# Weight rows shifted by 64 bytes each, two activation slots instead of three, and a signal after each bank of the first layer

## What is computed

```python
def _L0_ffn_ref(x, w1_w, w1_s, ...):          # 256 -> 1024 -> 1024 -> 1024 -> 256
    h = silu(tlin(x, w1_w, w1_s)) * tlin(x, w2_w, w2_s)
    h = gelu(tlin(h, h1_w, h1_s))
    h = gelu(tlin(h, h2_w, h2_s))
    return tlin(h, w3_w, w3_s)
x = x + 0.5 * ffn(layernorm(x))
x = x + attn(layernorm(x))                     # FFT convolution, gelu, @ W.T + b
x = x + 0.5 * ffn(layernorm(x))
```

## Time and profile before

| | |
|---|---|
| median of 3 runs | 1441.88 us (1441.57 to 1443.68) |
| the profiled execution, its own time | 1441.73 us |
| its span, first to last instruction | 1439.9 us |
| mean granted TensorE clock | 1.000 |
| busy: PE / PEld / DVE / ACT / POOL | 1432.2 / 1162.6 / 986.7 / 476.6 / 48.3 us |

### The profile page before, as it was taken

The page is one execution under the profiler, slowest core; times in us unless marked ns, Lnnn a source line. Parts: engine busy times, 40 slices in busy tenths (PEclk is TensorE's granted clock), DMA queues, the critical chain, the costliest instruction groups (busy, mean ns, idle before and its releaser), DMA issues.

```text
span 1439.9 us, 17283 instructions
## 1 busy us (share of the span) xinstructions
PE 1432.2 (99%) x6918; PEld 1162.6 (81%) x6918; DVE 986.7 (69%) x1736; ACT 476.6 (33%) x724; POOL 48.3 (3%) x42
## 2 busy tenths in 40 slices
PE   9999999999999999999999999999999999999999
PEld 4788888888778878788787878878878788888887
DVE  7867867675778887848878587784777754353433
ACT  5524342433324223233242232422424223141331
POOL 0000000000000000010000100001000010000000
PEclk9999999999999999999999999999999999999999
DMA  9000000012113221031210312012120112010000
GB/s 366 16 0 30 30 30 30 16 45 59 41 55 136 67 66 59 25 119 44 88 59 12 132 45 73 30 44 99 59 74 15 59 41 74 1 36 9 30 1 16
DMA packets 53906, 80.28 MB, mean 56 GB/s; under 512 B 2752, under 2 KB 45632, under 8 KB 52544
## 3 DMA queue, kind: packets, MB, share of 16 engines
q1 hardware_dynamic: 53824, 79.15, 16.2%
HBM read 57.12 MB, written 22.02 MB: 55 GB/s over the span
## 4 chain that ended last, share of the span: by engine, by line
PE 97%; DVE 2%; ACT 0%; issue 0%; POOL 0%; DVEq 0%
PE ps L1317 80%; PE ps L1391 8%; PE ps L1442 3%; PE ps L1495 2%; PE ps L1293 1%; PE ps L1436 1%; PE ps L1437 1%; PE ps L1404 1%; PE ps L1485 0%; DVE low L1176 0%; PE ps L1310 0%; DVE hid_b_lo L1211 0%; PE ps L1419 0%; PE ps L1427 0%; DVE hid_b_hi L1209 0%
## 5 line engine op out<-in xcount | busy, mean ns | idle before, releaser
L494 ACT ACTIVATE act_o<-ps,scales 128x512 f32<-128x512 f32 x384 | 264.6, 690 | 911.9 <-PE ps L1317 909.7
L1317 PE MATMUL ps<-hid_b_hi,h 128*128 128x512 f32 x1024 | 401.5, 392 | 0.5 <-DVE hid_b_lo L1211 0.5
L1317 PE MATMUL ps<-hid_b_lo,h 128*128 128x512 f32 x1024 | 398.7, 389 | 0.0
L1317 PE MATMUL ps<-hid_a_hi,h 128*128 128x512 f32 x992 | 391.0, 394 | 0.2
L1317 PE MATMUL ps<-hid_a_lo,h 128*128 128x512 f32 x992 | 386.4, 390 | 0.0
L1317 PEld LDWEIGHTS ps<-hid_b_hi,h 128*128 128x128 f32 x1024 | 192.2, 188 | 42.2 <-issue 1.2
L1317 PEld LDWEIGHTS ps<-hid_b_lo,h 128*128 128x128 f32 x1024 | 192.2, 188 | 40.7 <-issue 1.2
L1317 PEld LDWEIGHTS ps<-hid_a_hi,h 128*128 128x128 f32 x992 | 186.2, 188 | 45.7 <-DVE hid_a_lo L1202 2.4
L1317 PEld LDWEIGHTS ps<-hid_a_lo,h 128*128 128x128 f32 x992 | 186.2, 188 | 39.8 <-issue 2.2
L1317 PE MATMUL ps<-hid_b_hi,w 128*128 128x512 f32 x480 | 189.5, 395 | 0.0
L1317 PE MATMUL ps<-hid_b_lo,w 128*128 128x512 f32 x480 | 188.1, 392 | 0.0
(11 more groups left out here) (268 smaller groups left out, 1269.5 us busy)
## 6 DMA issues: line engine op xcount, KB each, us to landing
ks<-k_d SPq DMA_DIRECT2D x32, 512.0 KB, 3.9
raws<-in_weights SPq DMA_DIRECT2D x10, 1024.0 KB, 15.6
xin<-in_x SPq DMA_DIRECT2D x8, 512.0 KB, 3.9
x_d<-xin SPq DMA_DIRECT2D x8, 512.0 KB, 2.8
z_d<-xin SPq DMA_DIRECT2D x8, 512.0 KB, 2.8
zb<-z_d SPq DMA_DIRECT2D x8, 512.0 KB, 4.7
wb<-x_d SPq DMA_DIRECT2D x8, 512.0 KB, 4.1
x_d<-wb SPq DMA_DIRECT2D x8, 512.0 KB, 3.3
```

The source lines that it names most:

```text
L494: A(act_o[:, k % ACT_SLOTS], bank(source), func, scale=scale).then_inc(s_act, 1)
L1317: last = MM(o, weight[:, k, cols].bitcast(dt), part[:, k].bitcast(dt), start=(k == 0 and i == 0), stop=(k == n - 1 and i == len(act_) - 1))
```

## The change

1. **Rows.** h1, h2 and w3 get 16 more floats (SKEW, 64 bytes) per row, so that row k starts 64 k bytes further into a 512-byte line than row 0. hid_b, and all that lies behind it (xin, act_o, gz, zb, wb, fb, tt, ks, tables), starts 64 bytes into a line. w1, w2 and hid_a stay at line starts. Transfers, checks and roundings of the weights use rows instead of flat runs of 2,048 floats.
2. **Slots.** ACT_SLOTS goes from 3 to 2: ScalarE waits for the gate or split of k - 2.
3. **Signals.** TensorE raises a new semaphore s_half when the w1 bank of step m is full; ScalarE's silu waits for that and no longer for s_u. VectorE's gate waits for s_act and for s_u. TensorE's step m waits for s_act of m - 2 before its w1 product and for s_gate of m - 2 before its w2 product.

```diff
-ACT_SLOTS = 3
+ACT_SLOTS = 2
+
+SKEW = 16
...
+        shapes = {"w1": (KD, HID, 0), "w2": (KD, HID, 0), "h1": (KH, HID, SKEW), "h2": (KH, HID, SKEW), "w3": (KH, D, SKEW)}
...
+        *padded, W0 = zone(FRONT, *((n, [P, k, w + skew], F32R) for n, (k, w, skew) in shapes.items()))
+        r12, rh1, rh2, r3, _ = zone(
+            FRONT, ("raw_12", [P, 2 * KD, HID]), ("raw_h1", [P, KH, HID + SKEW]), ("raw_h2", [P, KH, HID + SKEW]),
+            ("raw_w3", [P, KH, D + SKEW]))
+        w1, w2, h1, h2, w3 = (t[:, :, 0:w] for t, (k, w, skew) in zip(padded, shapes.values()))
...
+        hid_a_hi, hid_a_lo, HB = zone(X0, ("hid_a_hi", [P, KH, TOK], F32R), ("hid_a_lo", [P, KH, TOK], F32R))
+        HB += 4 * SKEW
+        hid_b_hi, hid_b_lo, xin, act_o, gz, Z0 = zone(
...
+        def of_chunk(c, matrices):
+
+            for t in matrices:
+                n = t.shape[1] * t.shape[2] // CHUNK
+                if c < n:
+                    at = t.shape[1] // n
+                    return t[:, at * c:at * (c + 1)]
+                c -= n
+
+        def raw(c):
+            return of_chunk(c, (r12[:, :, :], rh1[:, :, 0:HID], rh2[:, :, 0:HID], r3[:, :, 0:D]))
...
-                    sp.dma_start(raws[:, chunk(c)], a["weights"][:, chunk(c)]).then_inc(s_w[c], 16)
+                    sp.dma_start(raw(c), by_rows(a["weights"][:, chunk(c)], c)).then_inc(s_w[c], 16)
...
             def hidden(T, k, func, scale):
-                act.wait_ge(s_u, at_u(T, k))
+                if k < KH:
+                    act.wait_ge(s_half, at_gate(T, k))
+                else:
+                    act.wait_ge(s_u, at_u(T, k))
...
-                A(place(c), raws[:, chunk(c)], ACT.Copy).then_inc(s_placed, 1)
+                A(place(c), raw(c), ACT.Copy).then_inc(s_placed, 1)
...
-                    V.tensor_tensor(low[:, :], low[:, :], words, ALU.bitwise_or).then_inc(s_low, 1)
+                    V.tensor_tensor(by_rows(low[:, :], c), by_rows(low[:, :], c), words, ALU.bitwise_or).then_inc(s_low, 1)
...
             def gate(T, m):
                 dve.wait_ge(s_act, at_u(T, m))
+                dve.wait_ge(s_u, at_u(T, m))
...
-                    pe.wait_ge(s_gate, at_gate(T, m - 2))
+                    pe.wait_ge(s_act, at_u(T, m - 2))
...
-                product(bank(o), w1 if T else first(0), cols, z_parts, KD, dt)
+                product(bank(o), w1 if T else first(0), cols, z_parts, KD, dt).then_inc(s_half, 1)
+                if m >= 2:
+                    pe.wait_ge(s_gate, at_gate(T, m - 2))
                 product(bank(o + 1), w2 if T else first(1), cols, z_parts, KD, dt).then_inc(s_u, 1)
```

More of the change, by code:

```diff
@@ L187, in zone @@
             return (*made, start)
[L189 to L196, removed]
+        shapes = {"w1": (KD, HID, 0), "w2": (KD, HID, 0), "h1": (KH, HID, SKEW), "h2": (KH, HID, SKEW), "w3": (KH, D, SKEW)}
+        scales, small, single, FRONT = zone(0, ("scales", [P, 4, KH]), ("small", [P, N_SMALL]), ("single", [P, 4]))
+        flag, expo, FRONT = zone(FRONT, ("flag", [P, 1], I32), ("expo", [P, J]))
+        FRONT += (-base - FRONT) % LINE
+        *padded, W0 = zone(FRONT, *((n, [P, k, w + skew], F32R) for n, (k, w, skew) in shapes.items()))
[3 more added lines that the diff above has]
+        w1, w2, h1, h2, w3 = (t[:, :, 0:w] for t, (k, w, skew) in zip(padded, shapes.values()))
         assert _ == W0
@@ L201, in build @@
         wmax = single[:, 3:4]
[L203 to L207, removed]
+        hid_a_hi, hid_a_lo, HB = zone(X0, ("hid_a_hi", [P, KH, TOK], F32R), ("hid_a_lo", [P, KH, TOK], F32R))
+        HB += 4 * SKEW
+        hid_b_hi, hid_b_lo, xin, act_o, gz, Z0 = zone(
+            HB, ("hid_b_hi", [P, KH, TOK], F32R), ("hid_b_lo", [P, KH, TOK], F32R), ("xin", [P, J, D]), ("act_o", [P, ACT_SLOTS, TOK]), ("gz", [P, J, D]))
         zf, low, _ = zone(HB, ("zf", [P, KD, TOK]), ("low", [P, CHUNK], I32))
@@ L252, in build @@
         s_bn, s_mv, s_stat, s_rstd, s_z, s_z2 = (sem(n) for n in ("s_bn", "s_mv", "s_stat", "s_rstd", "s_z", "s_z2"))
+        s_half = sem("s_half")
         s_zt, s_zhi, s_zlo, s_u, s_act, s_gate, s_ghi, s_glo, s_hi, s_split, s_o, s_upd, s_x = (sem(n) for n in (
@@ L283, in chunk, with by_rows @@
             return slice(c * CHUNK, (c + 1) * CHUNK)
-        def place(c):
[L286 to L292, removed]
+        def of_chunk(c, matrices):
[7 more added lines that the diff above has]
+            return of_chunk(c, (r12[:, :, :], rh1[:, :, 0:HID], rh2[:, :, 0:HID], r3[:, :, 0:D]))
+        def by_rows(flat, c):
+            return flat.rearrange("p (k n) -> p k n", k=raw(c).shape[1])
+        def place(c):
+            return of_chunk(c, (w1, w2, h1, h2, w3))
         @block.sync
@@ L306, in _ @@
                     sp.dma_start(scales[:, :, :], a["scales"]).then_inc(s_scales, 16)
-                sp.dma_start(by_columns(raws)[:, :, cols], by_columns(a["weights"])[:, :, cols]).then_inc(s_first[n], 16)
+                sp.dma_start(r12[:, :, cols], by_columns(a["weights"])[:, :, cols]).then_inc(s_first[n], 16)
             sp.dma_start(s3[:, :], a["w3_s"]).then_inc(s_const, 16)
@@ L322, in _ @@
                 for t in (w1, w2, h1, h2, w3):
-                    flat = t[:, :, :].rearrange("p k n -> p (k n)")
-                    sp.dma_start(flat.bitcast(F32), w_d[:, at:at + flat.shape[1]]).then_inc(s_raw, 16)
-                    at += flat.shape[1]
+                    n = t.shape[1] * t.shape[2]
+                    sp.dma_start(t.bitcast(F32), w_d[:, at:at + n].rearrange("p (k n) -> p k n", k=t.shape[1])).then_inc(
+                        s_raw, 16)
+                    at += n
                 sp.wait_ge(s_raw, 16 * 5)
@@ L1170, in check_weights @@
                     dve.wait_ge(s_w[c], 16)
-                words = raws[:, chunk(c)].bitcast(I32)
+                words = raw(c).bitcast(I32)
                 if c == 1:
-                    V.tensor_tensor(low[:, :], raws[:, chunk(0)].bitcast(I32), words, ALU.bitwise_or).then_inc(s_low, 1)
+                    V.tensor_tensor(by_rows(low[:, :], 0), raw(0).bitcast(I32), words, ALU.bitwise_or).then_inc(s_low, 1)
                 else:
                     dve.wait_ge(s_low, c - 1)
-                    V.tensor_tensor(low[:, :], low[:, :], words, ALU.bitwise_or).then_inc(s_low, 1)
+                    V.tensor_tensor(by_rows(low[:, :], c), by_rows(low[:, :], c), words, ALU.bitwise_or).then_inc(s_low, 1)
             def weigh_bits():
@@ L1333, in layer_one @@
                 else:
-                    pe.wait_ge(s_gate, at_gate(T, m - 2))
+                    pe.wait_ge(s_act, at_u(T, m - 2))
                 cols, o = slice(m * P, (m + 1) * P), 2 * (m % 2)
                 z_parts = (zhi, zlo) if T else (zf[:, :, :],)
-                first = lambda c: raws[:, chunk(c)].rearrange("p (k n) -> p k n", k=KD)
-                product(bank(o), w1 if T else first(0), cols, z_parts, KD, dt)
+                first = lambda c: raw(c)
+                product(bank(o), w1 if T else first(0), cols, z_parts, KD, dt).then_inc(s_half, 1)
+                if m >= 2:
+                    pe.wait_ge(s_gate, at_gate(T, m - 2))
                 product(bank(o + 1), w2 if T else first(1), cols, z_parts, KD, dt).then_inc(s_u, 1)
```

## The result

The changed kernel takes 1449.91 us (median of 4 runs, 1449.87 to 1449.98) against 1441.79 us: the ratio is 1.0053, 95% interval 1.0038 to 1.0068. It is slower by 8.1 us, where 5.9 less was forecast. The profiled execution has a span of 1448.1 us, at the same granted clock of 1.000.

The account below looks back on a forecast made before the run. TensorE, busy 1432.2 of 1439.9 us, was taken to bound the kernel. Signals saving 4.5 us in passes 1 to 15 and 1.4 in pass 0, all else 0, gave 5.9 less: 1436.0 us, range 1430 to 1444.

Parts of the forecast that it names:

- The shifted rows: TensorE's matmuls: 13.3 ns beyond column time seen as fixed weight-change cost; shift priced 0, bounds +48 and -75 us.
- crossing a line costs: Rival: h1 and h2 weight blocks straddling two lines load slower, 6.7 ns each, +24 us, 1460 us; chance 0.13.
- Floor falls: Rival: row phases remove part of each matmul's 13.3 ns; a quarter gives 1417 us, all 1361; chance 0.08.
- Signals, passes 1 to 15: First layer and start of h1: earlier gates end late weight loads, saving 0.31 us a pass, 4.5 us taken.
- Pass 0: Last low part, before TensorE's idle near 40 us, comes earlier with silu(7); 1.4 us saved, bounds 0 and 1.6.
- The added increments and waits: 128 more increments and 96 more waits on TensorE: 0, increments at most 6.4 us; VectorE's waits move earlier.
- the slots: ScalarE waiting for split or gate k - 2 delays nothing that TensorE needs soon: price 0, upper bound 0.
- the transfers and checks: Weight loads in shorter rows: 0, up to +1 us; checks and roundings with unchanged element counts: 0, up to +0.5.
- the parts add up: The sum: signal gains of 4.5 and 1.4 us, all else 0, give 5.9 us less.

Follow-up runs that it names:

- e2: The changed kernel with every shift at 0, keeping the new signals and two slots: 1434.71 us, ratio 0.9952 to the kernel before.
- e4: The changed kernel with weight rows unshifted, hid_b and what follows it still 64 bytes into a line: 1445.72 us, ratio 1.0029.
- e8: e2 with hid_b moved 448 bytes into a line, 64 before the next: 1453.95 us, ratio 1.0088.
- e9: Signals and two slots, each matrix at its own place: distances 128 in first layer, -32 in h1, 96 in h2, 128 for w3: 1466.12 us.
- e10: Like e9, with distances 32 in the first layer, 160 in h1, 128 in h2, 32 for w3: 1463.92 us, ratio 1.0157.
- e6: e2 with all weights, constants and activations together 64 bytes further, distances between operands unchanged: 1434.71 us, ratio 0.9954.
- e1: The kernel before with the new signals alone, three slots and no row shifted: 1434.64 us, ratio 0.9948.
- e5: The changed kernel with hid_b back at a line start, weight rows still shifted: 1447.71 us, ratio 1.0044.
- e11: Signals and two slots, everything at line starts except w3, 32 bytes into a line: 1431.88 us, ratio 0.9925.
- e12: Like e11, but with w3 224 bytes into a line: 1434.23 us, ratio 0.9945.

## Why the prediction was wrong

- **The step that failed** is "The shifted rows", with "I take 0": the shift costs 15.2 us on top of the new signals. Its argument was that an even pitch, the same 13.3 ns at two lengths, looks "like a fixed cost of changing weights, not like accesses that meet by address". The evenness came from the layout: all operands of before stood at distance 0 modulo 256, so their pitch could say nothing of the other distances. In the changed kernel pass 14 has 29.49 - 29.01 = 0.48 us more for h1 than e2, and 29.29 - 28.79 = 0.50 for h2. With 0.11 more in the first layer and 0.05 less in w3 that is 1.04 us a pass, 15.6 us in 15 passes, against the 15.2 of the medians. I had written that no row of this trace has a shifted operand; an unobserved price with bounds of -75 and +48 us should not have been given 0.64 of the chance on an argument of plausibility, nor a range of 14 us.
- **The rule of the Trainium skill** that I set beside it, "SBUF — State Buffer" (Who interferes with whom), by which TensorE's two read ports are independent, does not cover this: between e2 and e4, e8, e9 and e10 only the places of the tensors change, and the 512-column pitch of the layers whose distance changes grows by 2.3 to 7.5 ns. The measurement decides. The rule that other engines don't slow TensorE is not touched.
- **The rival "crossing a line costs"** had the side, and 3,584 matmuls x its 6.7 ns gave 1460. Its mechanism is refuted by e6. "Floor falls" came out in a small form that I had not priced: w3 alone, 256 columns, 3 ns.
- **Signals, passes 1 to 15:** right. In e1 the first layer and h1 of pass 14 take 14.53 and 29.01 us, 0.32 less than before (0.31 forecast). **Pass 0:** 1.4 forecast, and the check's product comes 1.54 earlier even on shifted rows. Together 6.8 measured by e1, 5.9 forecast.
- **The added increments and waits, the slots, the transfers and checks:** 0 forecast. e1 and e2 show 0 for the first three. Transfers and checks in rows with gaps have no run of their own, but pass 0 shows no cost: its h1 starts at 36.44 us in the kernel before and in the changed one, and VectorE's one wait for the weights is 4.1 and 4.3 us.
- **That the parts add up** was wrong too, though not decisive: signals and layout overlap by 2.8 us in the first layer and the start of h1.

**Open.** Why distance 64 gives 229.0 in h2 of e4 and 233.4 in its first layer, and 229 in the changed kernel's first layer, I can't say. In e4 the distances of the two layers are equal even modulo 4,096. Two readings show that the addresses of a layer's own operands don't settle its pattern: the two pitches at distance 128 (e10), and h1 of the changed kernel against h1 of e5. There hid_a and h1 lie at the same places in both kernels, and both have the same 16 intervals, but displaced by eight: 235.6 ns at the first matmul of a product and 224.0 at the ninth in one, 224.0 and 235.7 in the other. What picks the pattern, perhaps how the matmuls before it ran, is not shown, nor by what mechanism the two reads meet.

## What to carry to other kernels

Where TensorE streams 512 columns of one float32r operand and loads another for every matmul, put both at the same place modulo 256 bytes; which place it is did not matter for the two tried (0 and 64). A shift of 64 bytes here cost up to 6.7 ns on each 227. At 256 columns a difference of 32 bytes was the better one, so try it. An even pitch in a trace in which all operands are aligned is no evidence about unaligned ones, so a layout change deserves a run of its own, or a wide range, apart from the other parts of an edit. Signalling a bank as soon as it is full is worth it where a reader of the second bank is on the edge of being late: it gained 6.8 us, though the waits listed only 9.0 us in pieces of 0.2 under running matmuls.

## What the runs showed of the hardware

- The start-to-start time of 512-column float32r matmuls, each with its own weights, is 226.7 ns when streamed row and loaded block lie 0 or 256 bytes apart (modulo 512), and on average 229.0 to 234.2 ns at the seven other multiples of 32 below 256. Single intervals in the shifted layers run from 224 to 236 ns (changed kernel, h1). Being at a line start is worth nothing in itself (e6).
- For 256-column matmuls the sign turns: over the w3 layer 121.5 ns at distance 0 (e2), 118.4 at 32 (e10, e11), 120.1 at 224 (e12), 120.3 at 128 (e9).
- A weight load that is late stretches the pitch of the matmuls behind it too: in the kernel before, the load that is 0.20 us late at 1277.96 is followed by intervals of 278, 232, 231 and then 227 ns. With the waits satisfied 1.0 to 1.8 us before the product that they guard, the first layer went from 230.4 to 227.1 ns (e1).
